# Attention and mixture of experts in one kernel: a batch's eight row sends placed one by one between the normalisations

## What is computed

```python
x = x + _L0_xattn_ref(_layernorm(x), ctx_1024, Wq1, Wk1, Wv1, Wq2, Wk2, Wv2, alpha, Wout, bout)
x = x + _L0_ffn_ref(_layernorm(x), gate_w, w1, w3, w2)
# xattn: softmax(q2 k1') v1 and softmax(q1 k2') v2, mixed by sigmoid(alpha), then @ Wout + bout
# ffn: softmax of x @ gate_w', top 4 experts and their weights; silu(x w1) * (x w3) @ w2 of each, summed
```

## Time and profile before

| | |
|---|---|
| median of three runs | 2147.49 us |
| the profiled execution | 2151.62 us |
| its span, first to last instruction | 2149.9 us |
| TensorE matmuls busy | 1904.3 us (89%) |
| VectorE, ScalarE, GpSimd busy | 1388.3, 1233.6, 1222.7 us |
| GpSimd's sends (L575) | 248 from `routed`, 998 ns each |
| GpSimd's multiplies (L583) | 1024, 613 ns each |

### The profile page before, as it was taken

How to read it: one execution, slowest core, us unless ns; L and a number is a source line. 1 busy time by engine, 2 the same in 40 slices (tenths; PEclk the granted TensorE clock), 3 DMA queues, 4 the chain that set the end, 5 groups by cost and what they waited for, 6 DMA issues and landing times.

```text
span 2149.9 us, 51903 instructions
## 1 busy us (share of the span) xinstructions
PE 1904.3 (89%) x15782; PEld 1662.2 (77%) x15783; DVE 1388.3 (65%) x3231; ACT 1233.6 (57%) x3605; POOL 1222.7 (57%) x1688
## 2 busy tenths in 40 slices
PE   6899999999999999999999999997888988888400
PEld 5788888888888888888888888885788887888400
DVE  4567666666666766667776677768655545554398
ACT  5666666667666666666666666664444444444300
POOL 3356666656666666666666666666455555555400
PEclk9999999999999999999999999998999999999755
DMA  4331111111111111111111111117475444544399
GB/s 130 111 103 45 42 49 49 52 44 39 48 46 59 44 39 42 44 52 34 39 37 44 52 34 39 37 40 214 151 222 163 147 149 147 149 146 148 117 411 361
DMA packets 158561, 210.80 MB, mean 98 GB/s; under 512 B 24224, under 2 KB 131376, under 8 KB 158512
## 3 DMA queue, kind: packets, MB, share of 16 engines
q1 hardware_dynamic: 123696, 129.95, 19.8%
q0 software_dynamic: 26112, 71.86, 9.3%
q10 hardware_dynamic: 8704, 8.39, 1.1%
HBM read 113.02 MB, written 97.12 MB: 98 GB/s over the span
## 4 chain that ended last, share of the span: by engine, by line
PE 65%; DVE 9%; issue 7%; POOL 7%; DMA 5%; ACT 4%; another core or an unknown queue 2%; SPq 0%; ACTq 0%; POOLq 0%; DVEq 0%
PE p_pt L1366 10%; PE p_gu L1570 9%; PE p_s L1349 8%; PE p_av L1386 8%; PE p_s L1287 7%; PE p_x L1287 4%; DVE z_ahead L1254 4%; POOL x_rows L575 3%; PE p_y L1591 3%; POOL probs L583 3%; PE p_x L1417 3%; PE p_s L1297 3%; DMA x_rows<-routed,slot_i 2%; ACT probs L708 2%
## 5 line engine op out<-in xcount | busy, mean ns | idle before, releaser
L583 POOL TENSOR_TENSOR probs<-probs,inv 128x256 f32<-128x256 f32 x1024 | 596.9, 613 | 410.2 <-DVE inv L971 408.9
L708 ACT ACTIVATE probs<-p_s,nmx 128x256 f32<-128x256 f32 x1024 | 473.6, 481 | 74.4 <-PE p_pt L1366 43.4
L964 DVE TENSOR_REDUCE nmx<-p_s 128x4 f32<-128x1024 f32 x256 | 312.2, 1220 | 120.2 <-PE p_s L1349 120.2
L575 POOL DMA_INDIRECT x_rows<-routed,slot_i x248 | 247.4, 998 | 134.8 <-DVE target L956 70.5
L1366 PE MATMUL p_pt<-ident,probs 128*128 128x128 f32 x2048 | 292.8, 279 | 6.8 <-POOL probs L583 4.5
L1386 PE MATMUL p_av<-probsT,val 128*64 128x256 f32 x2048 | 259.2, 389 | 9.9 <-DVE probsT L859 7.0
L1366 PEld LDWEIGHTS p_pt<-ident,probs 128*128 128x128 f32 x2048 | 230.6, 142 | 40.1 <-issue 11.7
L696 ACT COPY probsT<-p_pt 128x512 f32<-128x512 f32 x256 | 151.3, 591 | 169.1 <-PE p_pt L1366 168.3
L859 DVE COPY probsT<-p_pt 128x512 f32<-128x512 f32 x256 | 176.0, 687 | 70.6 <-PE p_pt L1366 35.7
L708 ACT ACTIVATION_READ_ACCUMULATOR probs<-p_s,nmx 128x1 f32 x1024 | 216.4, 211 | 0.0
L1211 DVE TENSOR_TENSOR xgT_lo<-p_xt,xgT_hi 128x512 fp32r<-128x512 f32 x144 | 99.1, 688 | 176.8 <-ACT xgT_hi L816 151.0
(11 more groups left out here) (234 smaller groups left out, 5206.9 us busy)
## 6 DMA issues: line engine op xcount, KB each, us to landing
y_in<-y_rows SPq DMA_DIRECT2D x32, 1024.0 KB, 8.3
xg<-x_rows SPq DMA_DIRECT2D x72, 257.0 KB
xg_more<-x_rows SPq DMA_DIRECT2D x72, 257.0 KB
rows<-in_ctx_dram SPq DMA_DIRECT2D x32, 256.0 KB, 2.7
x_in<-in_x_dram SPq DMA_DIRECT2D x32, 256.0 KB, 2.9
mid_rows<-x_mid SPq DMA_DIRECT2D x32, 256.0 KB
x_rows<-bias SPq DMA_DIRECT2D x32, 256.0 KB, 3.4
z_ahead<-mid_rows SPq DMA_DIRECT2D x24, 256.0 KB
```

The costliest lines, as they stand in the source:

```text
L575: pool.indirect_dma_start(x_rows, bass.IndirectOffsetOnAxis(ap=slot_i[:, t, k:k + 1], axis=0), to_send[:, t, k, :], None).then_inc(last_se ...
L583: pool.tensor_tensor(pr[:, h, t, :], pr[:, h, t, :], rc[:, g:g + 1].to_broadcast([P, S]), ALU.mult).then_inc(normed_p, 1)
L708: act.activation(probs[u % 2][:, h, t, :], p_s[:, 2 * (u % 2) + h, t * S:(t + 1) * S], ACT.Exp, bias=nmx[u % 2][:, g:g + 1], accum_out=sum ...
L964: dve.tensor_reduce(nmx[i][:, :], p_s[:, 2 * i:2 * i + 2, :].rearrange("p h (t k) -> p (h t) k", t=ST), AX.X, ALU.max, negate=True).then_i ...
```

## The change

The same eight sends are placed one by one. Send 0 stands before the second half of step 7, sends 1 and 2 behind it, and sends 3, 4, 5 and 6 each behind one half of steps 0 and 1, whose normalisations are now called by halves. `x_res` and send 7 stay as they were. In the two iterations at the end of the stage, which have no batch of their own, `rsqrt` stays between sends 4 and 5.

```diff
@@ -596,21 +596,19 @@
                     pool.wait_ge(pads_filled, FILLED)
                     wait_alone(pool, router_step, ROUTER_STEPS * (b - 1))
                     wait_alone(pool, copies_set, b - 1)
-                    for i in range(2):
-                        send(i, to_send, last)
+                    send(0, to_send, last)
                 if prev and cur:
                     normalise(b - 1, STEPS - 1, (1,))
                 if old:
-                    for i in range(2, 5):
-                        send(i, to_send, last)
-                if cur:
-                    normalise(b, 0)
-                    normalise(b, 1)
-                if prev and not cur:
-                    rsqrt(norm2(b, cur))
-                if old:
-                    for i in range(5, 7):
-                        send(i, to_send, last)
+                    send(1, to_send, last)
+                    send(2, to_send, last)
+                for n in range(4):
+                    if cur:
+                        normalise(b, n // 2, (n % 2,))
+                    if prev and not cur and n == 2:
+                        rsqrt(norm2(b, cur))
+                    if old:
+                        send(3 + n, to_send, last)
                 if cur:
                     wait(pool, mid_set, b)
                     pool.wait_ge(x_landed, 16 * (b + 1))
```

## The result

The changed kernel takes 2188.8 us (median of four runs, 2186.7 to 2191.1) where the kernel before takes 2146.0 beside it: 1.0194 times as long, interval 1.0181 to 1.0207. That is 43 us slower; 27 were forecast. The profiled execution took 2191.1 us, its span is 2189.3. All of it lies in stage A: from the first send in the iteration of batch 2 to the first send in that of batch 32 it takes 1398.1 us, and 1355.6 in the profile of before, 42.5 more.

What follows compares the result with a forecast made beforehand. TensorE was taken to bound the attention stage. Fifteen early iterations at 1.0 us, thirteen late at 0.7 to 0.8 and two end ones at 1.0 gave 27 us: median 2174.5, own range 2163 to 2190, whole range 2160 to 2206.

Steps and rivals of the forecast that it cites:

- What bounds the kernel: Attention stage: TensorE is the bound, busy 539.44 of 540 us, so every gap it gets is paid in full.
- (1): Whole iteration: nothing is added or taken away; four more waits for `inv` are written, costed at nothing.
- (2): One send before step 7's second half instead of two: ready 1.3 us sooner, worth nothing, 2.4 us slack already.
- (3): Two sends instead of three before step 0: `inv` at 7.24 and start at 7.49, instead of 8.67 and 8.92.
- (4): Sends 3 to 6 between halves of steps 0 and 1: TensorE stands about 1.0 us, net loss 0.7 typically.
- (5): Everything behind steps 0 and 1: send 7 moves by 1.02 us to 18.64; step 2's delay is hidden.
- (6): Landing of send 7, before VectorE's L877: moves by 1.0 us, costs 1.0 us in early iterations, hidden in late ones.
- Rival A: Late signal stays, any nearby send delaying it: step 0 starts at 8.92; 68 us more, 2215 us; chance 0.15.
- B: Rival, faster: a half and its send take less than 2.39 us once alternated; 2134 us; chance 0.04.
- C: Rival, no measurable difference: reciprocal for step 0 before 6.9, fourth half ends by 15.5; about 2152 us; chance 0.08.
- The rule on the shared port: VectorE's L877 beside step 2's multiplies: up to 0.31 us per early iteration, 5 us over the kernel; charged nothing.

Runs made afterwards that it cites:

- changed_own_count: The changed kernel, with the two sends that read place 0 of `routed` first and on their own semaphore, which alone VectorE's normalisation awaits: 2183.1 us.
- own_count: The kernel before, with the two sends that read place 0 of `routed` first and on their own semaphore, which alone VectorE's normalisation awaits: 2120.4 us.
- front_two_one: The changed kernel with send 1 before step 7's second half instead of behind it: 2182.9 us, 1.0166 times the kernel before.
- step7_only: The kernel before with one send before step 7's second half and four in a row behind it: 2205.9 us, 1.0274 times the kernel before.
- row_broken: The kernel before with a small memset behind each of sends 2 and 3: 2149.5 us, 1.0009 times the kernel before.

## Why the prediction was right in direction and short in size

- *What bounds the kernel.* Right. TensorE is the bound of stage A, and what the change costs is gaps in it: 1.71 us an iteration in `changed_own_count` against `own_count`, whose TensorE is busy 540 of 540 us.
- *(1), (2) costs at nothing.* The added waits cost nothing: the spacing of half and send is 2.39 us (1072.63 to 1075.01), as worked out. But (2), "one send before step 7's second half instead of two", was priced as worth nothing, and this is the step that failed; it shows in (3). I looked only at step 7's second half, which has slack, and not at what send 1, one place later, does to the signal of the first half.
- *(3) `inv` of step 0.* The mis-sized term: 7.24 was taken, 7.87 measured, start 8.13 instead of 7.49. The late signal of step 7's second half did vanish (6.79 against 8.06), as argued. The one of the first half grew from 5.06 to 5.42. In the iteration of the earlier trace rows, from which I took the 7.24, ScalarE makes that copy at 4.79 (1399.35 less 1394.56), so its two signals were both on time, and I had asked this of one only. The stated other end, 8.67, did bound it. The measured time, 2188.8, lies just inside the forecast's own range (2163 to 2190), because both prices came out just above the 1.4 us that bound it: 1.42 and 1.49.

```profile
1399.35 0.59 ACT L696 COPY probsT<-p_pt 128x512 f32<-128x512 f32 x1 [1.35 <-PE p_pt L1366]
```

- *What is left without this term* can be seen in the changed kernel's iteration from 786.75. GpSimd happens to stand still in it for 2.28 us before its second send, both copies of step 7 are on time (4.79 and 6.53), and `inv` of step 0 comes at the forecast's 7.24:

```profile
791.32 1.02 POOL L575 DMA_INDIRECT x_rows<-routed,slot_i  x1 [2.28 <-issue]
792.64 0.96 POOL L575 DMA_INDIRECT x_rows<-routed,slot_i  x1 [0.30 <-issue]
794.26 1.18 POOL L583 TENSOR_TENSOR probs<-probs,inv 128x256 f32<-128x256 f32 x2 [0.65 <-DVE inv L969]
...
805.29 0.99 POOL L575 DMA_INDIRECT x_rows<-routed,slot_i  x1 [0.17 <-issue]
```

```profile
793.99 0.18 DVE L969 RECIPROCAL inv<-sums 128x4 f32<-128x4 f32 x1
```

```profile
801.20 0.60 PE L1364 MATMUL p_pt<-ident,probs 128*128 128x128 f32 x4
802.67 0.65 PE L1364 MATMUL p_pt<-ident,probs 128*128 128x128 f32 x4 [0.87 <-POOL probs L583]
```

From there everything is as forecast: step 0 starts at 7.51 (7.49), the last send at 18.54 (18.64), TensorE's gap is 1.04 us (1.0), and the iteration takes 46.05 us (46.1 to 46.4 for an early one).
- *(4) The stall at step 1.* Right in mechanism and in each spacing. From 8.13, three times 2.39 and 1.19 give 16.5; TensorE waits 1.6 us instead of 1.0. The late iterations lose 1.49 us (44.77 to 46.26) instead of 0.7.
- *(5), (6) The landing.* Send 7 starts at 19.17, not 18.64: the 0.64 us of the later start, less 0.1, since `x_res` follows the last send sooner than I had taken. The landing after it is as before (3.2 us in the late iterations and 4.2 in the early ones, means). Early iterations lose 1.42 us (45.41 to 46.83) instead of 1.0. That the stall decides late and the landing early is shown by `changed_own_count`: only the early ones get shorter.
- *Rival A* was right that a signal is still late, and wrong about which: step 7's second half is nearly on time, the first half is not. *B* and *C* are excluded by the same rows: the pair is 2.39 us, and `inv` never comes before 7.2.
- *The rule on the shared port* (the Trainium skill, SBUF — State Buffer, section Who interferes with whom) was charged at nothing, and the changed kernel gives no sign against that: L875 takes 0.73 or 0.74 us in the early iterations and 1.05 in the late one shown, as L877 in the earlier trace rows.

## What to carry to other kernels

When a queue waits in the middle of its order, what counts is how much work stands behind that wait and in front of the next piece that the bound engine needs. Here, spreading the sends evenly moved two of them past the wait. Before spreading, ask whether its deadline can be loosened: here two of eight transfers had a reader in a hurry, and counting them apart gave 0.56%. And look at every signal that falls due while a moved piece is at work or ends, the earlier ones too, not only at the one that it was moved past.

## What the runs showed of the hardware

Some of TensorE's completion signals come late while indirect sends are at work on GpSimd. On time means, by the earlier trace rows and their fellows, that the copy starts 0.64 to 0.70 us after the first of four transposes is issued. ScalarE's copy of step 7's first half is on time at 4.79 with no send near it, and comes at 5.06 with a send at 3.7 (the kernel before and `front_two_one`), at 5.42 with two at 2.45 and 3.77 (the changed kernel), and at 6.8 to 8.2 with four from 2.44 on (`step7_only`). In the waits of the kernel before, those with no releaser on record are both waits for TensorE's signals:

```profile
DVE probsT L859 <- remote: 28.7, 19, 1.5
ACT probs L708 <- remote: 10.9, 19, 0.6
```

What causes it stays open. `row_broken` excludes bare adjacency, and neither being near nor the number of sends decides. In `step7_only`'s iteration from 790.13 GpSimd stood still first and its row of four starts at 4.45; there both copies of step 7 are on time, at 4.79 and 6.53:

```profile
794.58 1.02 POOL L575 DMA_INDIRECT x_rows<-routed,slot_i  x1 [2.17 <-issue]
795.90 0.96 POOL L575 DMA_INDIRECT x_rows<-routed,slot_i  x1 [0.30 <-issue]
```

```profile
794.92 0.59 ACT L698 COPY probsT<-p_pt 128x512 f32<-128x512 f32 x1 [1.35 <-PE p_pt L1368]
```

The moment seems to. I counted, in batches 3 to 30 of all twelve profiles, the signal of the first maximum (due at 3.59) and those of step 7's halves (due at 4.79, and 0.64 us after the transposes), leaving out VectorE copies that stand behind a late maximum. A signal that fell due 0.9 to 1.2 us after the start of a send, as the send ends, was late in 417 of 425 cases; one that fell due within 0.35 us of the start of a send that directly followed another was late in all 102; of the other 342 none was. In the changed kernel the sends at 2.45 and 3.77 stand so to the signals due at 3.59 and 4.79. That is a pattern read afterwards from few distinct placings, and no run was made to test it.

Nor does the pair at 13.7 and 15.0 in the kernel before, behind eight multiplies, delay ScalarE's copy of step 1; it starts at 15.40, again 0.64 us after its transposes were issued (14.76):

```profile
1052.13 0.59 ACT L696 COPY probsT<-p_pt 128x512 f32<-128x512 f32 x1 [0.29 <-PE p_pt L1366]
```

VectorE's L877 takes 0.74 us alone and 1.05 us when it meets part of GpSimd's multiplies. In `own_count` it no longer waits for the landing, starts with them, and takes 2.39, while their own 2.37 us are those of the earlier trace rows:

```profile
1037.49 2.37 POOL L590 TENSOR_TENSOR probs<-probs,inv 128x256 f32<-128x256 f32 x4
1037.62 2.39 DVE L894 TENSOR_SCALAR routed<-x_mid,mv,rstd 128x256 f32<-128x256 f32 x2 [1.98 <-POOL rstd L576]
```

The Trainium skill says of such a pair that one shuts the other out of a shared port (SBUF — State Buffer, section Who interferes with whom), and these rows agree, with VectorE as the one that waits. It costs nothing here: TensorE is busy 540 of 540 us in that kernel's stretch.
